# Front stage of a graph and attention layer: one set of statistics for two norms, the condition moved into the key groups, keys and first window counts among the values

## The reference, cut to what matters

```python
xn = layernorm(x)                                   # eps 1e-5, no scale
x = x + gnn(xn, (src, dst), node_vec1, ...) + mix(xn, ...)
x = x + ffn(layernorm(x), ...)                      # 16 experts, top 2

# mix: linear attention with exponential features
h = layernorm(xn, g1, be1)                          # eps 1e-5, scale and shift
q, k, v = split(h @ Wqkv + bqkv)                    # 8 heads of 64, 256 features each
xn = xn + attention(q, k, v) @ Wproj + bproj
out = xn + gelu(layernorm(xn, g2, be2) @ W1 + b1) @ W2 + b2

# gnn: the condition of every node, then four layers of edge attention
ph = noise * arange(1, 33) * (2 * pi / 16)
emb = concat([sin(ph), cos(ph)])                    # 64 numbers a node
cond = silu(emb @ f_w1 + f_b1) @ f_w2 + f_b2        # 16 numbers a node
y = norm(x) * (1 + cond @ s_w + s_b) + cond @ b_w + b_b
```

## Time and profile before

| | |
|---|---|
| median of three runs | 2810.72 us |
| the profiled execution | 2810.99 us |
| its span | 2809.3 us |
| PE busy in the span | 2677.8 us (95%) |
| DVE, ACT, POOL busy | 1449.0, 852.6, 280.5 us |
| mean clock granted to PE | 0.983 |
| first feature product of the attention | at 243.51 us |

### The profile page before, as it was taken

One profiled execution on the slowest core, in us unless ns is written; L12 is line 12 of the kernel. 1 busy time (PEld: TensorE's weight loads), 2 busy tenths in 40 slices (PEclk: granted clock), 3 DMA queues, 4 the chain that ended last, 5 costly groups with the idle time before them and its releaser, 6 DMA issues. The chain is left out here.

```text
span 2809.3 us, 28866 instructions
## 1 busy us (share of the span) xinstructions
PE 2677.8 (95%) x10335; PEld 1616.2 (58%) x10336; DVE 1449.0 (52%) x3306; ACT 852.6 (30%) x1817; POOL 280.5 (10%) x303
## 2 busy tenths in 40 slices
...
DMA packets 104797, 203.78 MB, mean 73 GB/s; under 512 B 22033, under 2 KB 22243, under 8 KB 104655
## 3 DMA queue, kind: packets, MB, share of 16 engines
...
## 5 line engine op out<-in xcount | busy, mean ns | idle before, releaser
L1708 ACT ACTIVATE g_prob<-g_prob,g_row_max 125x1250 f32<-125x1250 f32 x160 | 214.0, 1337 | 710.6 <-DVE g_row_max L1642 710.6
L1448 PE MATMUL psum<-cols,w 128*128 128x500 f32 (+1 forms) x1152 | 408.7, 514 | 6.7 <-PEq L81 6.7
L1510 PE MATMUL psum<-g_k_cols,g_q_cols 128*125 128x512 f32 (+1 forms) x960 | 362.9, 513 | 1.9 <-DVE g_row_max L1639 1.9
L1524 PE MATMUL psum<-cols,rows 125*128 125x250 f32 x1600 | 364.0, 374 | 0.1
L1448 PEld LDWEIGHTS psum<-cols,w 128*128 128x128 f32 x1152 | 216.6, 190 | 186.8 <-issue 178.7
L1524 PEld LDWEIGHTS psum<-cols,rows 125*128 125x128 f32 x1600 | 302.6, 189 | 34.7 <-issue 3.8
L1639 DVE CUSTOM_DVE_ANT_0 g_prob<-psum,ln_count 125x1250 f32<-125x1250 f32 x160 | 233.4, 1459 | 74.1 <-PE psum L1510 74.1
L1510 PEld LDWEIGHTS psum<-g_k_cols,g_q_cols 128*125 128x125 f32 x960 | 168.0, 187 | 161.8 <-issue 159.2
L1649 DVE COPY cols<-psum 125x500 f32<-125x500 f32 x160 | 108.5, 678 | 198.0 <-PE psum L1539 198.0
L1539 PEld LDWEIGHTS psum<-ident,g_prob 125*125 125x125 f32 x1600 | 199.4, 188 | 9.0 <-issue 1.9
L1539 PE MATMUL psum<-ident,g_prob 125*125 125x125 f32 x1600 | 200.3, 272 | 0.0
...
## 6 DMA issues: line engine op xcount, KB each, us to landing
...
w<-in_L_gnn_m_w SPq DMA_DIRECT2D x8, 1024.0 KB
w<-in_L_mix_W SPq DMA_DIRECT2D x4, 1024.0 KB, 5.2
w<-in_L_gnn_wq SPq DMA_DIRECT2D x4, 1024.0 KB, 5.0
```

The lines of the kernel that those rows point to most:

```text
L1448: ins = c.pe.matmul(c.bank(group_bank(g), width), wt[:, k, o * 128:(o + 1) * 128], y_cols[:, k, start:start + width], start=(k == 0), stop ...
L1510: ins = pe.matmul(psum[0:P, start:start + width], q_cols[:, h, t * P:(t + 1) * P], k_cols[:, h, start:start + width], start=True, stop=True)
L1524: ins = pe.matmul(c.bank(6 + g % 2, 2 * P), v_rows[:, j, h * 128:(h + 1) * 128], turned_prob[:, g % 2, j, :], start=(j == 0), stop=(j == N ...
L1708: s.activation(prob[:, u, :], prob[:, u, :], ACT.Exp, bias=row_max[:, u, 1:2], accum_out=row_max[:, u, 2:3]).then_inc(exp_made, 1)
```

## The change

- **Statistics.** Only x's own are made, in three batches of tiles (0 to 1, 2 to 4, 5 to 9). From the variance v come the root of v + eps and the root of v + eps (v + eps); the reciprocal of the second norms x for h directly, since the variance of xn follows from v. The second statistics, roots and reciprocals of the head are gone. DVE makes the rows of h first (`h_first_dve`); ACT then makes xn in place (`x_norm_act`), with a scale and a bias.
- **Loads.** SP issues the odd x tiles right behind the edge ends, then the vectors, then the noise row. Each tile of xn is written in two pieces with a semaphore of its own; the key weights are issued behind the fifth tile, the query weights and the feature matrix behind the tenth.
- **Condition.** The three phase operations and the subtraction go to POOL, behind its gathers; the sine stands behind ACT's seventh tile; the hidden products go ahead of PE's groups 0 to 2, the gate to POOL, the condition's products ahead of groups 6 to 8, its eviction to ACT. The tensors are views of `ln_count` in place of `k_cols`.
- **Order.** The first two tiles' statistics stand ahead of DVE's window search and the first tile of h right behind it. `v_dve` works tile by tile; the keys stand between the values of tiles 2 and 3 on DVE and behind the sixth value tile on PE. Windows 0 and 1 are counted behind value tiles 8 and 9; the 24 groups carry two windows each.
- **Banks.** h turns in banks 4 and 5 in place of 6 and 7; the values ring in four banks, the groups in five, and the condition has bank 5.
- **z.** The first operand becomes the ratio of the two roots, and the second operation has no scalar.

```diff
-    X_AHEAD = 4
+    X_BATCHES = [(0, 2), (2, 5), (5, NT)]
+    V_RING = 4
+    QK_RING = 5
+    HIDDEN_AT, COND_AT = 0, 6
...
 def windows_in(i):
-    return range(i * BLOCKS // (2 * GROUPS), (i + 1) * BLOCKS // (2 * GROUPS))
+    return range(2 + i * (BLOCKS - 2) // (2 * GROUPS), 2 + (i + 1) * (BLOCKS - 2) // (2 * GROUPS))
...
 def sp_start():
     sp = c.sp
     load(sp, dst_i, a["dst"].rearrange("(c p e) -> p c e", c=C, e=P)).then_inc(dst_in, 16)
-    load(sp, noise, a["node_vec1"].rearrange("n a -> (n a)").partition_broadcast(2 * FREQ)).then_inc(noise_in, 16)
+    for t in range(1, NT, 2):
+        load_tile(sp, x[:, t, :], a["x"][t * P:(t + 1) * P, :], x_in[t])
+    for n, name in enumerate(("g1", "be1", "g2", "be2")):
+        load(sp, vec_rows[4 * n:4 * n + 4, :], by_rows(a["L0_mix_" + name])).then_inc(vecs_in, 16)
+    load(sp, vec_rows[16:24, :], by_rows(a["L0_mix_bqkv"][0:2 * D])).then_inc(vecs_in, 16)
+    load(sp, vec_rows[24:32, :], by_rows(a["L0_mix_b1"])).then_inc(vecs_in, 16)
+    load(sp, noise, a["node_vec1"].rearrange("(t n) a -> t (n a)", n=2 * P).partition_broadcast(
+        2 * FREQ)).then_inc(noise_in, 16)
...
-    for n, name in enumerate(("g1", "be1", "g2", "be2")):
-        load(sp, vec_rows[4 * n:4 * n + 4, :], by_rows(a["L0_mix_" + name])).then_inc(vecs_in, 16)
...
-    for t in range(1, NT, 2):
-        load_tile(sp, x[:, t, :], a["x"][t * P:(t + 1) * P, :], x_in[t])
     sp.wait_ge(outside_made, 1)
     load(sp, flag_dram[:, :], outside_i).then_inc(flags_out, 16)
...
-    for n, sem in ((1, wk_in), (0, wq_in)):
-        load(sp, w[n][:], wqkv[:, :, n * D:(n + 1) * D]).then_inc(sem, 16)
+    for t in range(NT):
+        sp.wait_ge(x_normed, t + 1)
+        load_tile(sp, xn_dram[t * P:(t + 1) * P, :], x[:, t, :], xn_out[t])
+        if t == 4:
+            load(sp, w[1][:], wqkv[:, :, D:2 * D]).then_inc(wk_in, 16)
+    load(sp, w[0][:], wqkv[:, :, 0:D]).then_inc(wq_in, 16)
     for r0 in (0, 64):
         load(sp, pmat[r0:r0 + 64, :], a["L0_mix_Pmat"]).then_inc(p_in, 16)
-    for t in range(NT):
-        sp.wait_ge(x_normed, t + 1)
-        load(sp, xn_dram[t * P:(t + 1) * P, :], x[:, t, :]).then_inc(xn_out, 16)
     sp.wait_ge(v_mm, NT)
     load(sp, w[2][:], chunks(a["L0_mix_Wproj"])).then_inc(wp_in, 16)
...
+    g.wait_ge(noise_in, 16)
+    g.wait_ge(freq_made, 4)
+    g.tensor_scalar(emb, noise, freq[:, 0:1], freq[:, 1:2], ALU.mult, ALU.add).then_inc(cond_step, 1)
+    g.wait_ge(cond_step, 1)
+    g.tensor_scalar(whole_turns, emb, ROUND, None, ALU.add).then_inc(cond_step, 1)
+    g.wait_ge(cond_step, 2)
+    g.tensor_scalar(whole_turns, whole_turns, -ROUND, None, ALU.add).then_inc(cond_step, 1)
+    g.wait_ge(cond_step, 3)
+    g.tensor_tensor(emb, emb, whole_turns, ALU.subtract).then_inc(turns_made, 1)
     g.wait_ge(h_turned, NT)
     g.memset(blank, 0.0).then_inc(blank_made, 1)
     g.wait_ge(blank_made, 1)
+    g.wait_ge(hidden_act, 6)
+    g.tensor_tensor(hidden, hidden, gate, ALU.mult).then_inc(hidden_made, 1)
...
     v.wait_ge(iotas_made, 7)
-    v.wait_ge(freq_made, 3)
-    v.tensor_scalar(freq[:, 0:1], freq[:, 0:1], 1.0 / 16.0, None, ALU.mult).then_inc(cond_step, 1)
-    v.wait_ge(cond_step, 1)
...
-    v.tensor_tensor(emb, emb, whole_turns, ALU.subtract).then_inc(turns_made, 1)
+    v.tensor_scalar(freq[:, 0:1], freq[:, 0:1], 1.0 / 16.0, None, ALU.mult).then_inc(freq_made, 1)
+    x_stats_dve(0)
+    x_stats_dve(1)
+    x_vars_dve(0)
     lowest, highest = (psum[0:BLOCKS, n * BANK:n * BANK + EDGE_TILES] for n in range(2))
...
+    x_scales_dve(0)
+    h_first_dve(0)
     v.wait_ge(first_sent, 1)
...
-def condition_pe():
+def condition_pe(at):
     pe = c.pe
-    pe.wait_ge(hidden_made, 1)
...
-def condition_dve():
-    v = c.dve
-    v.wait_ge(hidden_act, 6)
-    v.tensor_tensor(hidden, hidden, gate, ALU.mult).then_inc(hidden_made, 1)
...
+    if HIDDEN_AT <= at < HIDDEN_AT + 3:
+        i = at - HIDDEN_AT
+        pe.wait_ge(sin_made, 1)
+        pe.wait_ge(f_in, 64)
+        if i >= 1:
+            pe.wait_ge(hidden_act, 2 * i)
+        pe.matmul(by_span(c.bank(QK_RING, SPANS[i][1], COND)), f_w1[:, :],
+                  emb[:, noise_spans[i][0]:noise_spans[i][1], :], start=True, stop=True).then_inc(hidden_mm, 1)
+    if COND_AT <= at < COND_AT + 3:
+        i = at - COND_AT
+        pe.wait_ge(hidden_made, 1)
+        if i >= 1:
+            pe.wait_ge(cond_made, i)
+        pe.matmul(by_span(c.bank(QK_RING, SPANS[i][1], COND)), f_w2[:, :],
+                  hidden[:, noise_spans[i][0]:noise_spans[i][1], :], start=True, stop=True).then_inc(cond_mm, 1)
+def condition_act(at):
     s = c.act
-    s.wait_ge(turns_made, 1)
-    s.activation(emb, emb, ACT.Sin, scale=6.2831850).then_inc(sin_made, 1)
...
+    if HIDDEN_AT <= at < HIDDEN_AT + 3:
+        i = at - HIDDEN_AT
+        t0, t1 = noise_spans[i]
+        if i == 0:
+            s.wait_ge(f_in, 64)
         s.wait_ge(hidden_mm, i + 1)
-        s.activation(hidden[:, start:start + width], c.bank(4 + i % 2, width, COND), ACT.Identity,
+        s.activation(hidden[:, t0:t1, :], by_span(c.bank(QK_RING, SPANS[i][1], COND)), ACT.Identity,
                      bias=f_b[:, 0:1]).then_inc(hidden_act, 1)
-        s.activation(gate[:, start:start + width], c.bank(4 + i % 2, width, COND), ACT.Sigmoid,
+        s.activation(gate[:, t0:t1, :], by_span(c.bank(QK_RING, SPANS[i][1], COND)), ACT.Sigmoid,
                      bias=f_b[:, 0:1]).then_inc(hidden_act, 1)
+    if COND_AT <= at < COND_AT + 3:
+        i = at - COND_AT
+        start, width = SPANS[i]
+        s.wait_ge(cond_mm, i + 1)
+        s.activation(cond[0:COND, start:start + width], c.bank(QK_RING, width, COND), ACT.Identity,
+                     bias=f_b[:, 1:2]).then_inc(cond_made, 1)
...
+def sin_act():
+    c.act.wait_ge(turns_made, 1)
+    c.act.activation(emb, emb, ACT.Sin, scale=6.2831850).then_inc(sin_made, 1)
...
-def x_norm_dve(t):
+def x_vars_dve(b):
     v = c.dve
-    v.wait_ge(x_std, t + 1)
...
+    lo, hi = X_BATCHES[b]
+    v.wait_ge(x_mean, hi)
+    v.tensor_scalar(x_r[:, 0, lo:hi], x_mv[:, lo:hi, 1], EPS, None, ALU.add).then_inc(x_var, 1)
+    v.wait_ge(x_var, 2 * b + 1)
+    v.scalar_tensor_tensor(x_r[:, 1, lo:hi], x_r[:, 0, lo:hi], EPS, x_mv[:, lo:hi, 1], ALU.mult,
+                           ALU.add).then_inc(x_var, 1)
+def x_std_act(b):
+    lo, hi = X_BATCHES[b]
+    c.act.wait_ge(x_var, 2 * b + 2)
+    c.act.activation(x_r[:, 2:4, lo:hi], x_r[:, 0:2, lo:hi], ACT.Sqrt).then_inc(x_std, 1)
+def x_scales_dve(b):
     v = c.dve
-    stat, mv, rstd = h_stat_of(m)
+    lo, hi = X_BATCHES[b]
+    v.wait_ge(x_std, b + 1)
+    v.reciprocal(x_r[:, 4:6, lo:hi], x_r[:, 2:4, lo:hi]).then_inc(x_rstd, 1)
+    v.wait_ge(x_rstd, b + 1)
+    v.scalar_tensor_tensor(x_r[:, 6, lo:hi], x_mv[:, lo:hi, 0], -1.0, x_r[:, 4, lo:hi], ALU.mult,
+                           ALU.mult).then_inc(x_low, 1)
+    v.tensor_tensor(x_r[:, 7, lo:hi], x_r[:, 5, lo:hi], x_r[:, 2, lo:hi], ALU.mult).then_inc(x_ratio, 1)
+def x_norm_act(t):
+    s = c.act
+    s.wait_ge(x_low, 1 + (t >= X_BATCHES[1][0]) + (t >= X_BATCHES[2][0]))
+    s.wait_ge(normed, t + 1)
+    s.activation(x[:, t, :], x[:, t, :], ACT.Identity, bias=x_r[:, 6, t:t + 1],
+                 scale=x_r[:, 4, t:t + 1]).then_inc(x_normed, 1)
+def h_first_dve(t):
+    v = c.dve
+    if t >= H_RING:
+        v.wait_ge(h_turned, t - H_RING + 1)
+    v.tensor_scalar(h_rows[:, t % H_RING, :], x[:, t, :], x_mv[:, t, 0:1], x_r[:, 5, t:t + 1], ALU.subtract,
+                    ALU.mult).then_inc(normed, 1)
...
-        pe.wait_ge(cond_made, 3)
-    if t >= 6:
-        pe.wait_ge(v_made, t - 5)
+    if t >= V_RING:
+        pe.wait_ge(v_made, t - V_RING + 1)
     pe.wait_ge(h_cols, KC * (t + 1))
...
-    v.wait_ge(xn_out, 16 * NT)
+    v.wait_ge(xn_out[t], 32)
+    v.memset(slots[:, t, DH::DH + 1], 1.0).then_inc(v_ones, 1)
     v.wait_ge(v_mm, t + 1)
...
 def keys_pe():
     pe = c.pe
-    pe.wait_ge(h_cols, KC * NT)
     pe.wait_ge(keys_made, 2)
...
-        if i < 6:
-            pe.wait_ge(v_made, i + 7 if i + 6 < NT else i + 1)
-        elif i < GROUPS + 6:
-            pe.wait_ge(k_made, i - 5)
-        else:
-            pe.wait_ge(q_made, i - GROUPS - 5)
+        if i < 2:
+            pe.wait_ge(v_made, NT - 1 + i)
+        if i >= GROUPS + QK_RING:
+            pe.wait_ge(q_made, i - GROUPS - QK_RING + 1)
+        elif i >= QK_RING:
+            pe.wait_ge(k_made, i - QK_RING + 1)
+        condition_pe(i)
...
 def pe_start():
     start_pe()
-    condition_pe()
-    for t in range(NT + 1):
-        if t < NT:
-            h_turn_pe(0, t)
-        if t >= 1:
-            v_pe(t - 1)
-    keys_pe()
+    h_turn_pe(0, 0)
+    for t in range(NT):
+        if t + 1 < NT:
+            h_turn_pe(0, t + 1)
+        v_pe(t)
+        if t == 5:
+            keys_pe()
+        if t >= NT - 2:
+            sum_pe(t - (NT - 2))
     qkv_pe()
     attention_pe()
 def dve_start():
     v = c.dve
     start_dve()
-    for t in range(NT + X_AHEAD + 1):
```

(76 more changed lines are left out.)

122 lines of the change are left out of this document (42 added, 80 removed).

## The result

Before, in the same session, the kernel took 2811.93 us (four runs, 2810.43 to 2816.02); changed it took 2779.02 us (four, 2776.70 to 2782.78). The ratio is 0.9882, 95% interval 0.9865 to 0.9899: 33 us less. The profiled execution took 2776.70 us, span 2775.0.

What follows compares the result with a forecast made beforehand. Bounds: the chain of the norms, then DVE's one-hots. One-hots end at 200.6 + 2.7 + 0.8 + 2.8 = 206.9, first feature product 208.3 instead of 243.5; 2811.0 - 35.2 = 2775.8 us, range 2767 to 2788.

Steps and rivals of the forecast that it cites:

- When the first value tile starts: Head: first value product at 18.5 us instead of 44.45, 26 us earlier; ends 17.5 and 24.
- The value stage: Ten value tiles 40.55 us, key transposes 2.37, two windows 2.1; group 0 starts near 63.5 instead of 95.03.
- DVE keeps in front: Value stage: DVE makes the keys from 33.3 to 40.3, before PE asks for them at 44.2.
- The ring of four banks: Value stage: the four value banks ask for the sixth value near 59 and have it at 48.
- the ten tiles without a gap: Value stage, sign of being right: PE runs all ten value tiles without a gap.
- no gap of PE before the key transposes: Value stage, sign of being right: PE does not wait for the keys after the sixth value tile.
- Rival (a): Value stage: POOL holds DVE where keys are made, PE stalls 2.6 to 6.6, gate costs 4.2; 2782 us, chance 0.14.
- The group stage: Groups: DVE-bound, 46 windows at 2.865 us from 68.8 to 200.6, plus disturbances 2.7, condition 0.8, gate 2.8.
- The gate's own part: Groups: POOL's gate product holds DVE for its whole length, 2.8 us; ends 0 and 4.2.
- (b): Groups 0 to 2 and 6 to 8: PE cannot carry the condition, or first loads come late; 2784 us, chance 0.09.
- (c): Groups: PE held at its lower clock, 1.2 GHz, work taking 236 us; +63, 2874 us, chance 0.03.
- (d): Head is not what is waited for; a load or the slot fill holds 243; 2810 us, chance 0.02.

Runs made afterwards that it cites:

- c0: The changed kernel again, unedited, in the same set of runs as further edits: 2780.45 us, ratio 0.9873 to 0.9906 to the kernel before.
- c1: The changed kernel again, unedited, in another set of runs: 2778.28 us, ratio 0.9872 to 0.9902 to the kernel before.
- e7: Changed kernel with a second set of statistics, read by nobody, added on DVE for each first normed tile: 2781.69 us.
- e4: Changed kernel with the whole condition back at the head, ahead of the values, phases and gate on DVE, noise loaded early: 2791.20 us.
- e8: Changed kernel with DVE's first norms of tiles 5 to 7 held until POOL's phase operations are done: 2785.27 us, one run.
- e1: Changed kernel with the four phase operations on DVE instead of POOL, after the eighth normed tile: 2773.08 us.
- e9: Changed kernel with ACT making two instead of one of the nine one-hot parts of every other window: 2771.17 us.
- e6: Changed kernel with four more gate-sized POOL products behind the gate, on values nobody reads: 2789.97 us.
- e3: Changed kernel with the keys, their transposes and windows 0 and 1 back behind all ten value tiles: 2794.66 us.

## Why the prediction was right

**When the first value tile starts: right, 18.24 for 18.5, by the chain forecast but for its first link.** The forecast had the first tile of h at 15.4 and, separately, the small vectors "there by 15" and the weights at 17 to 19.5. The tile was ready at 14.24; PE's list puts the transposition of the vectors ahead of it, and that waited for their load until 15.16 (1.35 us; for the bytes ahead of it the text has 2.9 MB, the loads come to 2.7). From the vectors to v0 it took 3.1 us, where the text gives transposes and copies 2.9. v0 stands 3.07 or 3.08 us behind the vectors in the first profile, in c0 and in c1 (15.16, 15.04, 15.45), whether the last wait is put down to the weights or, in c0 and c1, to ACT's copies. So the weights come in together with the copies and are not seen to delay v0. e7 shows that the single set of statistics, as far as DVE's work goes, brings v0 forward by nothing; the removed stretch (phases, gate, condition) brings most of the 26.2, as e4 shows by putting it back (+23.1). Whether an earlier load of the vectors would bring v0 forward, or the weights would then hold it, no run tried.

**The value stage: right in sum, 46.0 for 45.0, by errors that cancel.** The ten tiles took 40.3 (forecast 40.55), the windows 2.0 (2.1); in both kernels that holds one slow tile, the first (6.17 and 5.72 us for the 3.60 of later ones), for which the rows show no lower clock. The key transposes cost 1.2 and not 2.37, for the row of before that priced them stood behind a pause of 7.9 us and so at the lower clock. Against that, PE paused 2.5 us where the text said "with PE asking for them at 44.2" and the keys ready at 40.3. This is the step that failed: "DVE keeps in front" was walked without POOL in it, and the forecast put that hold at nothing. The keys were ready at 46.0, 45.5 and 45.4 in the three profiles, and PE asked for them earlier than forecast, at 42.8 in c0 (six tiles of 4.055 from 18.5 give 42.8 too, not 44.2), so the slack was 2.5 us and not 3.9. The ring of four banks was walked only at its last turn; the first profile's other pause is at its first, where the fifth tile wants the first bank back. Two of the prediction's own signs of being right, "the ten tiles without a gap" and "no gap of PE before the key transposes", did not come in the first profile. In c0 the same pause came in one piece, the clock fell, and the transposes did take 2.40.

**Rival (a), POOL holds DVE where the keys are made: its mechanism is there, its size was too large in most runs.** POOL's phases took 11.2 us (7 to 11 forecast, up to 15 if stretched, which e8 excludes). PE's stalls were 2.5, 2.7 and 2.4 us, at the lower end of the rival's 2.6 to 6.6, and 2.2 to 5.0 us of the value stage with the clock (e1); the gate held DVE for 2.16 us where the rival said 4.2 and the forecast 2.8. In c0 4.3 us of the hold fell on the norms and 4.0 on the keys, near the half of the argument against it. The forecast and this rival were not exclusive: the true course was the forecast with the rival's first half in it. The time doesn't part them either: 2779.0 lies 3.2 us above the forecast and 3.0 below the rival's 2782, and that it is inside the range is owed in part to errors of opposite sign.

**The group stage: 143.9 for 144.8.** The one-hots were bound by DVE (e9). Window 4 began at 69.81 for 68.8, behind the count of window 2. DVE's timeline there:

```profile
67.03 0.28 DVE L778 TENSOR_SCALAR p_shared<-iota,edge_cols 125x250 f16<-125x250 f16 x1
69.81 0.26 DVE L776 TENSOR_SCALAR p_shared<-iota,edge_cols 125x125 f16<-125x125 f16 x1 [2.50 <-PE psum L801]
```

The last one-hot ended at 206.81 for 206.9, so the 46 windows took 137.0: 131.8 undisturbed and 5.2 of disturbances, for which 6.3 was set (2.7 + 0.8 + 2.8). The gate's own part was mis-sized: 2.16 (2.41 - 0.25) for 2.8, since POOL's product took 2.47. The products of the condition cost DVE 1.4 (0.6 in the first three groups, 0.8 in the second set) for 0.8, and some 1.6 is left for the memsets and the rest where 2.7 was taken over. That each of POOL's operations is paid whole, not by the 1.15 of 2.49 that the memsets cost, was right: e6 gave 2.49 for each.

**The rest moved as a block: right** within 1.0 us in the first profile (2566.8 for 2565.8); the experiments lie between 2564.5 and 2569.6.

**The medians.** The profiled run gained 34.3 us (2811.0 to 2776.7) against 35.2 forecast. The medians gained 32.9, and 30.0 and 32.4 in the repeats c0 and c1, whose profiles show the fall of the clock. That fall, 1.4 to 2.6 us at F, stood in no term of the sum.

**How the gain divides.** Put back one at a time, the condition at the head (e4), the keys and first counts behind the values (e3) and the second statistics (e7) move F by 14.6, 14.8 and 4.7 us against the first profile, 34.1 of its 35.3, and by 12.0, 12.2 and 2.1 against c0, 26.3 of its 32.7. That the parts add is not shown; by either count the condition and the keys are most of it.

**Rivals (b), (c), (d).** (b) is small: PE's pairs of windows with a condition product took 6.43 us for 5.73 (70.67 from 64.24), but only the first three and the three from 101.83 on, and DVE waited for it 0.6 and 0.8 us. (c) did not occur: granted clock 0.98 in the groups. (d) did not: every edit that moved v0 or K0 or took work off DVE moved F and the time with it, e7's time the least.

What stays open: which course (one pause or two) an unprofiled run takes and how often, and what shifts DVE against POOL by the tenths that decide it. Why POOL's two operations with an immediate take 3.4 us where the one with operands from memory takes 1.4 was not tried; they also do one arithmetic step where it does two.
